# Layer 1 attention: all sixteen query-key products of a group on VectorE

## The reference, cut to what matters

```
qkv = jnp.einsum('sbf,pf->sbp', src, in_proj_weight) + in_proj_bias
q, k, v = jnp.split(qkv, 3, axis=-1)
q = to_heads(q) / np.sqrt(d)          # d = 64
k = to_heads(k)
v = to_heads(v)
attn = jnp.einsum('nsd,ntd->nst', q, k)
attn = jax.nn.softmax(attn, axis=-1)
out = jnp.einsum('nst,ntd->nsd', attn, v)
...
out = out @ out_proj_weight.T + out_proj_bias
```

## Time and profile before

| | |
|---|---|
| median of 3 runs | 2418.3 us (2417.81 to 2419.02) |
| the profiled execution | 2418.87 us |
| its span, first to last instruction | 2417.1 us |
| busy in the span: PE, DVE, ACT, POOL | 2027.0, 1616.6, 1121.6, 938.3 us |
| layer 1 attention in the span | 555 to 909 us |
| first product of VectorE, softmax of group 0 | 569.2 us, 613.7 us |

### The profile page before, as it was taken

How to read it: one execution, slowest core, us unless ns; L and a number is a source line. 1 busy time by engine, 2 the same in 40 slices (tenths; PEclk the granted TensorE clock), 3 DMA queues, 4 the chain that set the end, 5 groups by cost and what they waited for, 6 DMA issues and landing times. The chain is left out here.

```text
span 2417.1 us, 35796 instructions
## 1 busy us (share of the span) xinstructions
PE 2027.0 (84%) x12728; PEld 1406.0 (58%) x12728; DVE 1616.6 (67%) x2541; ACT 1121.6 (46%) x2142; POOL 938.3 (39%) x728
## 2 busy tenths in 40 slices
PE   7889849978899965877899799988899986599993
PEld 4556639962344444554566565655566564499992
DVE  5687745445878874888888877888788884322224
ACT  3333211103744653656666476656676672133332
POOL 3233232323113200455576456564576572222222
PEclk9999969988999987989999899999999998699997
DMA  3110035210000002000000000000000000531113
GB/s 148 37 37 21 10 144 206 91 57 18 1 1 1 0 1 90 1 1 1 28 1 1 10 28 1 1 10 1 1 1 1 10 1 9 221 134 36 38 34 113
DMA packets 36714, 93.29 MB, mean 39 GB/s; under 512 B 5415, under 2 KB 24379, under 8 KB 31934
## 3 DMA queue, kind: packets, MB, share of 16 engines
q1 hardware_dynamic: 30462, 74.72, 8.6%
q0 software_dynamic: 6080, 16.29, 2.0%
HBM read 76.56 MB, written 14.44 MB: 38 GB/s over the span
## 5 line engine op out<-in xcount | busy, mean ns | idle before, releaser
L1965 POOL TENSOR_TENSOR x_total<-x_total,x_pt 128x1024 f32<-128x1024 f32 x186 | 439.2, 2361 | 198.4 <-ACT x_pt L2024 182.4
L2045 ACT ACTIVATE x_pt<-PS,x_maskf 128x512 f32<-128x512 f32 x544 | 332.2, 687 | 180.8 <-PE PS L2313 177.8
L2127 DVE TENSOR_TENSOR PS<-x_pt,PS 128x512 f32<-128x512 f32 x480 | 333.2, 694 | 74.8 <-ACT x_pt L2045 36.8
L2284 PE MATMUL PS<-x_pt,x_vs 128*64 128x256 f32 x2176 | 286.1, 404 | 77.9 <-ACT x_pt L2024 72.1
L2145 DVE TENSOR_TENSOR x_pt<-x_pt,PS 128x1024 f32<-128x1024 f32 x320 | 320.4, 1051 | 0.7 <-PE PS L2331 0.7
L2024 ACT ACTIVATE x_pt<-x_pt 128x1536 f32<-128x1536 f32 (+1 forms) x160 | 266.1, 1664 | 50.6 <-DVE x_pt L2145 50.4
L2313 PE MATMUL PS<-x_qs,x_ks 64*128 64x256 f32 x2176 | 282.0, 395 | 1.9 <-ACT x_pt L2045 1.9
L2284 PEld LDWEIGHTS PS<-x_pt,x_vs 128*64 128x64 f32 x2176 | 153.8, 143 | 205.8 <-ACT x_pt L2024 78.0
L1143 PEld LDWEIGHTS PS<-m_xT,m_own 128*128 128x128 f32 x1984 | 235.5, 195 | 7.4 <-DVE m_own L1219 3.3
L1143 PE MATMUL PS<-m_xT,m_own 128*128 128x128 f32 x1984 | 236.4, 278 | 3.2 <-DVE m_own L1219 2.8
L2313 PEld LDWEIGHTS PS<-x_qs,x_ks 64*128 64x128 f32 x2176 | 199.5, 189 | 65.7 <-issue 40.2
(11 more groups left out here) (269 smaller groups left out, 2861.1 us busy)
## 6 DMA issues: line engine op xcount, KB each, us to landing
f_w<-in_L_ffn_w SPq DMA_DIRECT2D x32, 1024.0 KB, 6.3
a_ctxT<-in_ctxT SPq DMA_DIRECT2D x8, 800.5 KB, 4.4
f_w<-ys SPq DMA_DIRECT2D x24, 256.0 KB, 5.9
x_cx<-in_ctx SPq DMA_DIRECT2D x4, 1536.0 KB
l_w<-in_L_attn_w SPq DMA_DIRECT2D x6, 512.0 KB
a_xT<-in_xT SPq DMA_DIRECT2D x4, 512.0 KB, 5.2
X<-in_x SPq DMA_DIRECT2D x1, 2048.0 KB, 11.1
xr<-a_xn SPq DMA_DIRECT2D x16, 128.0 KB, 1.7
```

The lines of the kernel that those rows point to most:

```text
L1965: ins = nc.gpsimd.tensor_tensor(total2[:], first, tile[:, 2 * k + 2:2 * k + 4, :], ALU.add)
L2045: nc.scalar.activation(pt[:, s % 2, t, :].rearrange("p (h n) -> p h n", h=2), PS[:, first:first + 2, half], ACT.Identity, bias=maskf[:, b ...
L2127: ins = nc.vector.tensor_tensor(acc, tile, acc, ALU.max)
L2284: mm = nc.tensor.matmul(PS[h * HDX:(h + 1) * HDX, AVB, 0:QN], vs[:, p % 2, t, h * HDX:(h + 1) * HDX], pt[:, u % 2, t, h * QN:(h + 1) * QN] ...
```

## The change

VectorE makes all sixteen products, alternating between the two buffers of `l_prod`, and all sixteen sums go by L1576 with a token of `chain`. The buffer `l_pp` and the semaphores `pp_ready` and `pp_used` go. GpSimd keeps the initial memset and `rstd`, now called once for each group in order and waiting for nothing but `mv_ready`.

```diff
-        pp = sb("pp", [P, P1])
...
-        POOL_PAIRS = (2, 5, 8, 11, 14)
-        NP = len(POOL_PAIRS)
...
             for grp in range(J):
-                for k, i in enumerate(POOL_PAIRS):
-                    s, t = PAIRS[i]
-                    pool.wait_ge(ring_free, grp * USES + TURNED + 4 * (max(s, t) + 1))
-                    if grp * NP + k >= 1:
-                        pool.wait_ge(pp_used, grp * NP + k)
-                    nc.gpsimd.tensor_tensor(by_head(pp[:]), heads(grp, s, 0), heads(grp, t, 1), ALU.mult).then_inc(pp_ready, 1)
-                    if k == 0 and grp >= 2:
-                        rstd(pool, grp - 2)
-            rstd(pool, J - 2)
-            rstd(pool, J - 1)
+                rstd(pool, grp)
...
-                if i in POOL_PAIRS:
-                    k = POOL_PAIRS.index(i)
-                    dve.wait_ge(pp_ready, grp * NP + k + 1)
-                    nc.vector.reduce_sum(sc[:, grp % 2, s, t, :], by_head(pp[:]), AX_X).then_inc(pp_used, 1)
-                else:
-                    dve.wait_ge(chain, product)
-                    token(nc.vector.reduce_sum(sc[:, grp % 2, s, t, :], by_head(prod[:, own(i) % 2, :]), AX_X))
+                dve.wait_ge(chain, product)
+                token(nc.vector.reduce_sum(sc[:, grp % 2, s, t, :], by_head(prod[:, i % 2, :]), AX_X))
...
-                    if i < B * B and i not in POOL_PAIRS:
-                        if own(i) >= 2:
+                    if i < B * B:
+                        if i >= 2:
                             dve.wait_ge(chain, n[0])
                         s, t = PAIRS[i]
                         dve.wait_ge(ring_free, grp * USES + TURNED + 4 * (max(s, t) + 1))
-                        if grp >= 1 and own(i) < 2:
+                        if grp >= 1 and i < 2:
                             dve.wait_ge(own_ready, grp * B)
                         product[i] = token(nc.vector.tensor_tensor(
-                            by_head(prod[:, own(i) % 2, :]), heads(grp, s, 0), heads(grp, t, 1), ALU.mult))
+                            by_head(prod[:, i % 2, :]), heads(grp, s, 0), heads(grp, t, 1), ALU.mult))
...
-                dve.wait_ge(pp_used, (grp + 1) * NP)
```

More of the change, by code:

```diff
@@ L1413, in layer1_attention @@
         ring_done, ring_free = sem("ring_done"), sem("ring_free")
-        pp_ready, pp_used, sc_ready, ex_ready, attn_ready = sem("pp_ready"), sem("pp_used"), sem("sc_ready"), sem("ex_ready"), sem("attn_ready")
+        sc_ready, ex_ready, attn_ready = sem("sc_ready"), sem("ex_ready"), sem("attn_ready")
         own_ready, wp_ready, third_added, o_ready = sem("own_ready"), sem("wp_ready"), sem("third_added"), sem("o_ready")
@@ L1569, in score @@
                 s, t = PAIRS[i]
-                if i in POOL_PAIRS:
-                    k = POOL_PAIRS.index(i)
-                    dve.wait_ge(pp_ready, grp * NP + k + 1)
-                    nc.vector.reduce_sum(sc[:, grp % 2, s, t, :], by_head(pp[:]), AX_X).then_inc(pp_used, 1)
-                else:
-                    dve.wait_ge(chain, product)
-                    token(nc.vector.reduce_sum(sc[:, grp % 2, s, t, :], by_head(prod[:, own(i) % 2, :]), AX_X))
-            def own(i):
-                return i - sum(p < i for p in POOL_PAIRS)
+                dve.wait_ge(chain, product)
+                token(nc.vector.reduce_sum(sc[:, grp % 2, s, t, :], by_head(prod[:, i % 2, :]), AX_X))
             def first_two(grp, s):
```

## The result

Over 20 runs each, the changed kernel takes 2422.3 us in the median (2420.2 to 2429.45) and the kernel before 2419.05 us (2417.63 to 2420.12). The ratio is 1.0018, with a 95% interval of 1.0011 to 1.0025: slower by 4.4 us (2.7 to 6.1), less than the 0.2% that the prediction took as its bound. The medians differ by 3.25 us; the forecast was 3.2 us more and 2421.5 us, counted from a median of 2418.3 us of three runs of before. In the experiments three executions in a slower state (2746, 3061 and 3467 us, at a mean granted clock of 0.55 to 0.73; two of before, one of e10) are left out. The profiled execution of the changed kernel takes 2420.99 us, with a span of 2419.3 us.

What follows compares the result with a forecast made beforehand. No engine was simply full, so waits between engines decide. Group 0 adds 3.16 us and groups 1 to 3 add 0: 2418.3 + 3.2 = 2421.5 us, range 2419.0 to 2425.0.

Steps and rivals of the forecast that it cites:

- Group 0: In the first group of the stage, VectorE reaches the softmax 3.16 us later, all of it passed on.
- The price of a product: On VectorE, each product moved from GpSimd costs 1.36 us; 20 cost 27.2 us if nothing else changed.
- the stalls: VectorE products, adds and normalizations slowed by GpSimd's products in the four groups; removing these gives back 15.9 us.
- TensorE's longer idle stretch: Ahead of group 1, TensorE's idle time grows from 2.22 to 5.4 us; added cost 0 or 1.55, taken as 0.
- Group 1: VectorE's softmax comes 2.0 us later there, and its wait for value chunks shrinks from 5.76 to 3.7 us; cost 0.
- ScalarE's thin margin at part 24: In group 1, VectorE's `add` ends 1.1 us before ScalarE needs it, so ScalarE is not held.
- Groups 2 and 3: There, 5.3 us of removed stalls pay for the five moved products; cost 0 in each.
- The slack is spent: Rival: slack in groups 1 to 3 runs out, stopping ScalarE, then TensorE; 2423.5 us, up to 2429.6; chance 0.14.
- No cost: Rival: group 0's lateness is taken up later, say by ScalarE's waits before `turned`; 2418.3 us, chance 0.06.
- Faster: Rival: in groups 1 to 3 the stalls are on the path, the added products not; 2407.7 us, chance 0.04.
- the size of the noise: Runs of the kernel before were taken to differ by 1.2 us, which helped set the forecast's low end.

Runs made afterwards that it cites:

- e10: e6 run again without an edit; time ratio to the kernel before 0.9987 (0.9979 to 0.9996), 3.1 us less.
- e1: The changed kernel run again without an edit; time ratio to the kernel before 1.0010 (1.0001 to 1.0020).
- e2: Kernel before with GpSimd's five products moved to VectorE in group 0 alone; time ratio to before 1.0011 (1.0002 to 1.0020).
- e7: Kernel before with two of group 0's GpSimd products (pairs 11 and 14) moved to VectorE; time ratio to before 1.0012 (1.0004 to 1.0021).
- e5: Kernel before, with GpSimd's product of pair 5 waiting for VectorE's product of pair 4; time ratio to before 0.9996 (0.9987 to 1.0004).
- e6: e5 with ScalarE making group 0's exponential ahead of its last value copy; time ratio to the kernel before 0.9990 (0.9982 to 0.9999).
- e4: Changed kernel, with ScalarE making two copies of group 1 ahead of group 0's exponential; time ratio to the kernel before 1.0010 (1.0001 to 1.0019).
- e8: Changed kernel with two more pairs of products and sums on VectorE in groups 1 to 3; time ratio to the kernel before 1.0038 (1.0025 to 1.0051).
- e9: e6 with all products of groups 1 to 3 on VectorE; time ratio to the kernel before 0.9992 (0.9983 to 1.0000).

## Why the prediction was right

**Group 0 (+3.16 us).** Measured +3.26 from P0 to S0, three times within 0.01 (after, e1, e2). A pair takes 2.39 us, not 2.38, twelve times. Passing it on was right too: the first `add` still ends ScalarE's wait (3.12 us, 3.30 before), and e2 lengthens the stage by 2.9 us with only group 0 changed, where the two profiles of the full change have 3.4 and 3.0.

**The price of a product (1.36) and the stalls.** e7 measures 1.33 by itself. The stalls gave back 15.6 us of VectorE's busy time (products 8.5, `add` 3.0, normalizations 4.1), where the sum has 15.9. That a stall of GpSimd is worth its 2.2 us where it is on the path, e5, e6 and e10 show: 2.07 at the softmax, and all of it in the stage once ScalarE's order lets it through. The stage's 3.0 and 3.1 us hold 0.6 and 1.1 us of shorter projections besides.

**TensorE's longer idle stretch.** I had bounds of 0 and 1.55 us and took 0. It became 5.46 us (5.4 foretold). One chunk was slow, as before, not two, and taking the stretch away in e4 gained nothing.

**Group 1 (2.0 us later, absorbed).** S1 is 2.1 us later in the group's own time (72.60 from S0, before 70.49); the wait is 3.76 against the 3.7 foretold. ScalarE's thin margin at part 24 held: the one wait of ScalarE for an `add` is the 3.12 us of group 1, as before. **Groups 2 and 3**: waits of 2.65 and 2.67 us against the 2.6 and 2.7 foretold.

**The rivals.** "The slack is spent" did not happen, but e8 shows that the cover is limited and that the price then grows faster than I put it: 4.8 us more on VectorE in each group use up the waits, and 7.3 us are paid where 5.2 were not covered. "No cost" is excluded by the interval. "Faster" also: the Trainium skill (GPSIMD Engine Reference, Engine selection), which sends such products to VectorE, has the durations right (1.22 against 2.35 us), but GpSimd's time was not on the path. What made GpSimd's products nearly free is in the same skill (SBUF — State Buffer, Who interferes with whom): a `tensor_reduce` never contends with GpSimd, a VectorE instruction with two inputs in SBUF does when GpSimd reads SBUF. The trace agrees: beside GpSimd's products sums keep 1.21 us, and a product that starts just behind one of GpSimd's rises to 3.40.

**What was only nearly right** is the size of the noise. I took 1.2 us from three runs. The 95% interval of the change, 2.7 to 6.1 us, has its middle at 4.4 while the stage has 3.0 to 3.4; five of the first 20 runs, at 2424.9 to 2429.5 us, pull it up. That the medians differ by 3.25 us, so close to the 3.2 of the forecast, is in part luck: for the same two kernels e1 has a ratio of 1.0010, 2.4 us. The forecast's high end of 2425.0 holds the median, and not four of those runs.

## What to carry to other kernels

Price an instruction by the step it adds at the next place where engines meet: here the same five products cost 3.3 us in the group whose scores feed a waiting engine and nothing in the three groups where VectorE waits afterwards anyway (and in two of these the stalls that went paid for the products). A helper engine's product that runs beside sums is nearly free, even at twice the duration, and one that starts just before a product of the main engine costs it nearly the helper's whole length; moving the helper's start behind that product gained time, where removing the helper's products lost time. Look next to such a gain for an instruction queued ahead of the one released (ScalarE's last copy), or the gain stays there.

## What the runs showed of the hardware

After an idle stretch TensorE runs at the lower of its two granted clocks for a while, and how long differs between executions of the same work. The first projection of group 1, sixteen matmuls behind 4.35 to 5.5 us of idle time, takes 4.26 us in e10, 4.96 in after, 5.60 in e4 and 5.93 in e9; the next projections take 3.72 in all of them. In e9 and then e10 TensorE's row just before it shows the same idle time:

```profile
661.10 1.94 PE L1692 MATMUL PS<-ident,l_o 128*128 128x128 f32 x8 [4.35 <-ACT l_oT L1495]
```

```profile
660.84 1.94 PE L1693 MATMUL PS<-ident,l_o 128*128 128x128 f32 x8 [4.35 <-ACT l_oT L1494]
```

The granted clock is 0.50 (1.2 GHz) up to 667.0 us in e9, while in e10 it is already 1.00 (2.4 GHz) from 665.0 us on. This work is on the path: the first projections differ by up to 1.7 us in group 1, 0.8 in group 2 and 0.4 in group 3, and so do the stretches. After 0.87 us of idle time (e4) and after 1.17 (e5) the next chunk is not slow at all; after 2.22 us it is, at a granted clock of 0.55.

Layer 0 differs too, ahead of anything that was changed: P0 lies between 568.69 and 576.77 us in the profiled executions. The stretches 80 to 95 and 110 to 135 us of before and of e4 (busy PE, PEld, DVE, ACT, POOL, then the clock):

```profile
80.00:95.00 15.00, 12.88 (x112) 7.44 (x112) 12.43 (x27) 7.01 (x11) 1.54 (x3) 1.00 0.18 56
...
110.00:135.00 25.00, 22.97 (x153) 15.19 (x152) 17.85 (x40) 6.00 (x12) 8.33 (x12) 1.00 0.02 7
```

```profile
80.00:95.00 15.00, 12.44 (x96) 7.13 (x96) 9.66 (x21) 5.33 (x9) 0.86 (x3) 0.77 0.17 55
...
110.00:135.00 25.00, 23.11 (x158) 14.28 (x162) 13.72 (x32) 4.20 (x8) 7.40 (x12) 0.88 0.01 4
```

The clock is 1.00 and 1.00 in the one, 0.77 and 0.88 in the other, and P0 is 7.0 us later in e4, whose profiled run took 2429.3 us. That accounts for most of this high run. A late P0 goes with a long run elsewhere as well: the profiled run of e6 (P0 at 576.77) lies 5.8 us over the median of its kernel, that of e5 (568.69) 5.0 under. That the clock makes P0 late is likely and not shown, since between 95 and 110 us it is the kernel before that has the lower one (0.89, e4 0.98). None of this settles why the first 20 runs of before held none: later runs of before go up to 2425.5 and 2426.5 us, and no profiled execution of the changed kernel itself was a high one, so whether the change makes them more frequent stays open.
